# First expert stage of a two-layer graph network: inner units interleaved over the blocks, mixing weights repeated over partitions by a transfer

## The reference

```python
tw = _routing_weights(xf, Wr, br, Wgate, bgate)      # 16 weights of a node, most of them 0
out = jnp.zeros_like(xf)
for e in range(E):                                   # E = 16
    h = jax.nn.silu(xf @ W1[e]) * (xf @ W3[e])       # 32 inner units of one expert
    out = out + tw[:, e:e + 1] * (h @ W2[e])
```

## Time and profile before

| | |
|---|---|
| median of 3 runs (lowest, highest) | 2427.51 us (2425.49, 2428.58) |
| profiled execution: run, span | 2430.37 us, 2428.6 us |
| PE busy over the span | 2278.6 us (94%) |
| DVE, ACT, POOL busy | 1795.1 (74%), 1152.4 (47%), 676.4 (28%) |
| mean granted TensorE clock | 0.969 of 2.4 GHz |
| from 500 to 1100 us: PE, DVE, ACT busy of 600 us | 600.00, 502.08, 317.68 |

### The profile page before, as it was taken

One profiled execution on the slowest core, in us unless ns is written; L12 is line 12 of the kernel. 1 busy time (PEld: TensorE's weight loads), 2 busy tenths in 40 slices (PEclk: granted clock), 3 DMA queues, 4 the chain that ended last, 5 costly groups with the idle time before them and its releaser, 6 DMA issues. The chain is left out here.

```text
span 2428.6 us, 33166 instructions
## 1 busy us (share of the span) xinstructions
PE 2278.6 (94%) x10610; PEld 1824.9 (75%) x10610; DVE 1795.1 (74%) x4258; ACT 1152.4 (47%) x2136; POOL 676.4 (28%) x624
## 2 busy tenths in 40 slices
PE   6799986899999999999789999999997899999998
PEld 4577664688888888888668788888876677777776
DVE  8588796888888888887556755555566688888886
ACT  7565422445455454554442222222235767667652
POOL 6455022222122221210232222122133434333310
PEclk9899987999999999999899999999999899999999
DMA  5221133132231322311453343433446566666631
GB/s 168 57 54 53 19 126 104 57 100 83 75 104 53 105 70 87 102 51 52 135 173 126 125 145 127 134 129 128 135 157 195 123 174 160 148 169 166 152 106 51
DMA packets 155873, 271.89 MB, mean 112 GB/s; under 512 B 35538, under 2 KB 36178, under 8 KB 155478
## 3 DMA queue, kind: packets, MB, share of 16 engines
q1 hardware_dynamic: 123014, 203.00, 25.1%
q0 software_dynamic: 32720, 67.19, 12.9%
HBM read 185.82 MB, written 100.41 MB: 118 GB/s over the span
## 5 line engine op out<-in xcount | busy, mean ns | idle before, releaser
L2417 ACT ACTIVATE conv_h<-conv_h 128x512 f32<-128x512 f32 x79 | 50.0, 632 | 305.9 <-DVE conv_h L2346 288.8
L2894 POOL DMA_INDIRECT next_own<-message,net_slot_d x75 | 123.7, 1650 | 155.4 <-DMA next_own<-own 138.1
L2315 DVE TENSOR_TENSOR conv_yl<-conv_pty,conv_yh 128x512 fp32r<-128x512 f32 x79 | 54.6, 692 | 150.2 <-ACT conv_yh L2407 140.9
L67 PE MATMUL conv_p<-conv_w_hi,conv_yh 128*128 128x512 f32 x316 | 132.2, 418 | 1.2 <-DVE conv_yl L2315 1.2
L1372 POOL TENSOR_TENSOR d_rs<-d_ve,net_half_neg 128x4 f32<-128x4 f32 x37 | 37.3, 1008 | 340.8 <-DVE d_ve L1430 283.4
L67 PE MATMUL d_po<-shared_wq_hi,d_hh 128*128 128x512 f32 x316 | 129.4, 409 | 0.0
L67 PE MATMUL d_pc<-d_xh,shared_wv_hi 128*128 128x512 f32 (+1 forms) x320 | 128.4, 401 | 0.0
L67 PE MATMUL d_pa<-d_xh,xp_w_hi 128*128 128x512 f32 (+1 forms) x320 | 127.6, 399 | 0.0
L69 PE MATMUL conv_p<-conv_w_hi,conv_yl 128*128 128x512 f32 x316 | 126.2, 399 | 0.0
L68 PE MATMUL conv_p<-conv_w_lo,conv_yh 128*128 128x512 f32 x316 | 126.0, 399 | 0.0
L69 PE MATMUL conv_p<-conv_w_hi,conv_hl 128*128 128x512 f32 x316 | 125.5, 397 | 0.0
(11 more groups left out here) (621 smaller groups left out, 7209.5 us busy)
## 6 DMA issues: line engine op xcount, KB each, us to landing
conv_yin<-y SPq DMA_DIRECT2D x79, 256.0 KB, 2.8
h<-conv_h SPq DMA_DIRECT2D x79, 256.0 KB, 2.0
own<-xp_own_buf SPq DMA_DIRECT2D x79, 256.0 KB, 2.0
next_own<-own SPq DMA_DIRECT2D x79, 256.0 KB, 4.3
next_x<-y SPq DMA_DIRECT2D x79, 256.0 KB, 3.8
out<-d_res SPq DMA_DIRECT2D x79, 256.0 KB, 2.7
y<-d_y SPq DMA_DIRECT2D x78, 256.0 KB
d_x<-in_x SPq DMA_DIRECT2D x10, 1024.0 KB, 7.3
```

Source lines behind the costliest of these rows:

```text
L67: te.matmul(out, lhs[0], rhs[0], start=first, stop=False, skip_group_check=True)
L2315: v.tensor_tensor(lo[:, t % 2, :], bank[t % 2][:], hi[:, t % 2, :].bitcast(F32), ALU.subtract)\
L2417: act_.activation(h[:, t, :], h[:, t, :], ACT.Relu).then_inc(h_made, 1)
L2894: pool.indirect_dma_start(own[n][:, t, :], None, k.message2[:, :], bass.IndirectOffsetOnAxis(ap=k.slot["d"][:, T * g + t:T * g + t + 1], a ...
```

## The change

Inner units are dealt out anew: block `cc` now holds units `8cc` to `8cc+7` of every one of the 16 experts, so partition `p` of every block belongs to expert `p // 8`. The columns of `e_w1`, `e_w3` and the rows of `e_w2` are put into that order by the host before the launch (`interleaved`). One 128 x 512 tile of weights, `mix_wide`, then serves all four blocks of a group. It is made so: DVE writes `mix` with 32 places for a tile; PE turns it with one transpose (before, two); ACT copies the 16 x 128 pieces of the four tiles from four quadrants of `d_ptr` to 16 partitions, `mix_rows`, times 0.25 (four copies in place of two); SP starts a transfer that writes each of the 16 rows to 8 partitions of `mix_wide` (`widen_mix`), and DVE multiplies with that tile out of SBUF instead of the bank `d_pmix` (`scale_mix`, split off from `scale_gate`). Gone are `spread` and its bank, the constants `expert`, `expert2`, `expert_r`, and the high and low `parts` of the weights. In block 0 the product with the weights is moved behind the low part of the next group's tile 0.

```diff
+PER = P // EXPERTS0
...
-        mix = c.sb("mix", [P, T, EXPERTS0])
-        parts = c.sb("parts", [P, T, HALF_P], F32R)
-        mix_t = c.sb("mix_t", [P, GR], F32R)
+        mix = c.sb("mix", [P, T, QUAD])
+        mix_rows = c.sb("mix_rows", [EXPERTS0, GR])
+        mix_wide = c.sb("mix_wide", [P, GR])
...
+            def widen_mix(g):
+
+                sp.wait_ge(hidden, KC * g + 2)
+                sp.wait_ge(mix_out, T * g + T)
+                rows = mix_rows[:, cols(g)]
+                sp.dma_start(mix_wide[:, cols(g)], rows.unsqueeze(1).broadcast_to([EXPERTS0, PER, rows.shape[1]]))                  .then_inc(mix_in, 16)
...
+                if c_ and in_range(i, c_, 0):
+                    widen_mix(i * XS + c_)
...
             load(2, 2)
+            widen_mix(0)
             sp.wait_ge(w2_low, 1)
             load(3, 3)
...
-            def constants():
-                s(pool.memset(expert[:], 0.25))
-                s(pool.memset(expert2[:], 0.25))
...
                 v.tensor_tensor(h, h, pc[cc % 2][:, cols(g)], ALU.mult).then_inc(gated, 1)
+
+            def scale_mix(g, cc):
+                h = act_out[:, cc % 2, cols(g)]
                 v.wait_ge(gated, 8 * g + 2 * cc + 2)
-                v.wait_ge(mixed, 4 * g + cc + 1)
-                v.tensor_tensor(h, h, pmix[:, cols(g)], ALU.mult).then_inc(hidden, 1)
+                v.wait_ge(mix_in, 16 * g + 16)
+                v.tensor_tensor(h, h, mix_wide[:, cols(g)], ALU.mult).then_inc(hidden, 1)
...
-                link(ins)
-                v.wait_ge(mix_turned, g + 1)
-                link(v.tensor_copy(parts[:, :, 0:EXPERTS0], mix[:]))
-                s(v.tensor_tensor(parts[:, :, EXPERTS0:2 * EXPERTS0], mix[:], parts[:, :, 0:EXPERTS0].bitcast(F32),
-                                  ALU.subtract))
+                s(ins)
...
                 chunk(g, 0)
                 if mid:
                     low(g + 1, n1, 0)
+                scale_mix(g, 0)
                 low_hidden(g, 0)
...
-            v.wait_ge(consts, 8)
-            v.tensor_tensor(expert_r[:], expert[:], expert2[:], ALU.add).then_inc(expert_made, 1)
-            v.wait_ge(expert_made, 1)
-            v.tensor_copy(expert_r[HALF_P:HALF_P + 2 * EXPERTS0], expert_r[0:2 * EXPERTS0].bitcast(F32)).then_inc(expert_made, 1)
+            v.wait_ge(consts, 2)
...
                 act_.wait_ge(mix_turned, g + 2)
-                for b in range(2):
-                    act_.activation(tile_pairs(mix_t, b)[pair_rows[b]], ptr[pair_rows[b], 0:2 * P].rearrange("p (a n) -> p a n", a=2),
-                                    ACT.Copy).then_inc(mix_out, 1)
+                if g:
+                    act_.wait_ge(hidden, KC * g + 2)
+                for t in range(T):
+                    act_.activation(mix_rows[:, t * P:t * P + P], ptr[t * QUAD:t * QUAD + EXPERTS0, 0:P], ACT.Copy, scale=0.25)\
+                        .then_inc(mix_out, 1)
...
-                if name == "w1":
-                    pe.wait_ge(hidden, 4 * g + cc + 1)
+                if name == "w1" and g + cc > 1:
+                    pe.wait_ge(gated, 8 * g + 2 * cc - 2)
...
-            def spread(g, cc):
-                pe.wait_ge(hidden, 4 * g + cc + 2)
-                pe.matmul(pmix[:, cols(g)], expert_r[:, cc * P:cc * P + P], mix_t[:, cols(g)], start=True, stop=True).then_inc(mixed, 1)
...
-                for a_ in range(2):
-                    last = pe.transpose(ptr[:, a_ * P:a_ * P + P],
-                                        parts[:, 2 * a_:2 * a_ + 2, :].rearrange("p t n -> p (t n)").bitcast(F32), k.ident[:])
-                last.then_inc(mix_turned, 1)
+                pe.transpose(ptr[:, 0:P], mix[:].rearrange("p t n -> p (t n)"), k.ident[:]).then_inc(mix_turned, 1)
...
+    def interleaved(v):
+
+        return v.reshape(D, EXPERTS0, KC, PER).transpose(0, 2, 1, 3).reshape(D, -1)
...
-        "e_w1": np.asarray(L0_ffn_W1).transpose(1, 0, 2).reshape(D, -1),
-        "e_w3": np.asarray(L0_ffn_W3).transpose(1, 0, 2).reshape(D, -1),
-        "e_w2": np.asarray(L0_ffn_W2).reshape(-1, D),
+        "e_w1": interleaved(np.asarray(L0_ffn_W1).transpose(1, 0, 2)),
+        "e_w3": interleaved(np.asarray(L0_ffn_W3).transpose(1, 0, 2)),
+        "e_w2": interleaved(np.asarray(L0_ffn_W2).transpose(2, 0, 1)).T,
```

More of the change, by code:

```diff
@@ L1260, in dense0_phase @@
         wins, ties = (c.sb(n, [P, NS, 4, 4]) for n in ("wins", "ties"))
[L1261 to L1263 removed]
+        mix = c.sb("mix", [P, T, QUAD])
+        mix_rows = c.sb("mix_rows", [EXPERTS0, GR])
+        mix_wide = c.sb("mix_wide", [P, GR])
         pa, pc, po = ([c.ps(f"{n}{i}") for i in range(2)] for n in ("pa", "pc", "po"))
[L1265 removed]
+        ptr = c.ps("ptr")
         turn_bank = [ptr, pa[0], pa[1], pc[0]]
@@ L1272, in dense0_phase @@
         place_made, slots_out, slots_in = c.sem("place_made"), c.sem("slots_out"), c.sem("slots_in")
-        consts, router_made, expert_made, routed_in = (c.sem(n) for n in ("consts", "router_made", "expert_made", "routed_in"))
+        consts, router_made, routed_in = (c.sem(n) for n in ("consts", "router_made", "routed_in"))
+        mix_in = c.sem("mix_in")
         w2_in, w2_high, w2_low = early.weight_in[2], early.weight_high[2], early.weight_low[2]
@@ L1284, in dense0_phase @@
         turned, xh_made, xl_made = (c.sem(n) for n in ("turned", "xh_made", "xl_made"))
-        up_done, gate_done, mixed, tanh_done = (c.sem(n) for n in ("up_done", "gate_done", "mixed", "tanh_done"))
+        up_done, gate_done, tanh_done = (c.sem(n) for n in ("up_done", "gate_done", "tanh_done"))
         gated, hidden, hh_made, hl_made = (c.sem(n) for n in ("gated", "hidden", "hh_made", "hl_made"))
@@ L1293, in dense0_phase @@
         block = stack.enter_context(nc.Block(no_gpsimd_drain=True))
-        NSTAT, NROUTE = 4, 26
+        NSTAT, NROUTE = 4, 24
         SET4 = SETS * 4
@@ L1403, in _ @@
                 gather(1, t)
-            constants()
             power(1, 1)
@@ L1439, in constants @@
                     v.memset(wr[:, :, b * HALF_P + 2 * SET4:(b + 1) * HALF_P].bitcast(F32), 0.0).then_inc(router_made, 1)
-                    v.memset(tile_pairs(mix_t, 1 - b)[pair_rows[b]].bitcast(F32), 0.0).then_inc(router_made, 1)
                 v.tensor_copy(wr[:, :, HALF_P:HALF_P + 2 * SET4], wr[:, :, 0:2 * SET4].bitcast(F32)).then_inc(router_made, 1)
-                v.memset(parts[:, :, 2 * EXPERTS0:HALF_P].bitcast(F32), 0.0).then_inc(router_made, 1)
+                v.memset(mix[:, :, EXPERTS0:QUAD], 0.0).then_inc(router_made, 1)
             def front0_begin(i, c_):
@@ L1590, in routing @@
                 sets = prob[:].rearrange("p (t s) e -> p t s e", t=T)
+                v.wait_ge(mix_turned, g + 1)
                 for t in range(T):
-                    ins = v.tensor_tensor(mix[:, t, :].rearrange("p (s e) -> p s e", e=4), sets[:, t, 1:SETS, :],
+                    ins = v.tensor_tensor(mix[:, t, 0:EXPERTS0].rearrange("p (s e) -> p s e", e=4), sets[:, t, 1:SETS, :],
                                           sets[:, t, 0, :].unsqueeze(2).broadcast_to([P, 4, 4]), ALU.mult)
-                link(ins)
-                v.wait_ge(mix_turned, g + 1)
-                link(v.tensor_copy(parts[:, :, 0:EXPERTS0], mix[:]))
-                s(v.tensor_tensor(parts[:, :, EXPERTS0:2 * EXPERTS0], mix[:], parts[:, :, 0:EXPERTS0].bitcast(F32),
-                                  ALU.subtract))
+                s(ins)
                 assert s.n == NROUTE
@@ L1669, in body @@
                 scale_gate(g, 1)
+                scale_mix(g, 1)
                 low_hidden(g, 1)
@@ L1679, in body @@
                 scale_gate(g, 2)
+                scale_mix(g, 2)
                 if front:
@@ L1689, in body @@
                 scale_gate(g, 3)
+                scale_mix(g, 3)
                 if front and tiles(g + 2) == T:
@@ L1869, in _ @@
             pe.sem_inc(mix_turned, 1)
-            pe.wait_ge(router_made, 6)
+            pe.wait_ge(router_made, 4)
             def turn(g, t, first=False):
@@ L1877, in turn @@
                 elif not first:
-                    pe.wait_ge(mix_out, 2 * g)
+                    pe.wait_ge(mix_out, T * g)
                 for kc in range(KC):
@@ L1937, in body @@
                     turn_mix(0)
-                    pe.wait_ge(expert_made, 2)
-                    pe.wait_ge(mix_out, 2)
-                    spread(0, 0)
                     turn(1, 0)
@@ L1946, in body @@
                     up(g, n, 0, "w3", pc, gate_done)
-                    pe.wait_ge(mix_out, 2 * g + 2)
-                    spread(g, 0)
                     if mid:
@@ L1954, in body @@
                     up(g, n, 1, "w3", pc, gate_done)
-                spread(g, 1)
                 if mid:
@@ L1961, in body @@
                 up(g, n, 2, "w3", pc, gate_done)
-                spread(g, 2)
                 up(g, n, 3, "w1", pa, up_done)
@@ L1966, in body @@
                 up(g, n, 3, "w3", pc, gate_done)
-                spread(g, 3)
```

3 lines of the change are left out of this document (removed).

## The result

| | before | after |
|---|---|---|
| median (lowest, highest) | 2427.54 us (2425.49, 2428.58) | 2449.05 us (2447.04, 2449.52) |
| ratio, 95% interval | | 1.0087 [1.0074, 1.0099] |
| profiled execution: run, span | 2430.37, 2428.6 us | 2449.52, 2447.7 us |
| 500 to 1100 us: PE, DVE, ACT busy | 600.00, 502.08, 317.68 | 576.67, 483.91, 306.92 |

The account below looks back on a forecast made before the run. PE bounds the stage, DVE close behind. 17 groups at +0.31 us (+5.3), group 18 -0.3, start +0.5, last group +2.9 sum to +8.4 us: 2435.9, rounded 2436, against the median 2427.51; range 2414 to 2446.

Parts of the forecast that it names:

- PE's gain: On PE, four `spread` products and one transpose go: -0.99 us a group; 0.40 comes back through DVE, net -0.59.
- L: Time of the weights' transfer from SP's issue to landing, taken as 3.55 us, the middle of 2.8 and 4.3.
- the slow case: Slow end of the likeliest case: L = 4.3, ACT's copies 1.3; +0.9 us more a group, some 2452 us.
- the prediction's own chain: Weights 0.90 us late at DVE's block 0 product delay tile 1's low part, then PE: +0.31 us a group.
- Lateness is paid in full: DVE is in-order, so all 0.90 us of the weights' lateness goes into the group: -0.59 + 0.90 = +0.31 us.
- The two stalls: PE waits for DVE at tile 2's transposes, 0.44 us, and at tile 2 of `down`, 0.86 us.
- the prediction's own sign: A period off 37.7 us plus the weights' lateness would mean that DVE's slack was wrong.
- The ends of the stage: Start +0.5 us, group 18 -0.3, last group +2.9, where nothing covers the transfer.
- The transfer under the cover: Rival: with L between 2.0 and 2.8 the weights come in time; -10.4 us, so 2417; chance 0.30.
- Far slower: Rival: eightfold reading makes L = 7.3, weights 4.65 us late, +4 us a group, 2500 or more; chance 0.06.
- DVE alone as the bound: Rival: DVE, not PE's starts, bounds the stage, so removing products on PE gives nothing; no chance of its own.
- The break-even: The whole change, its last group counted, breaks even at about L = 3.1.

## Why the direction was right and the size was not

**What bounds the kernel, and PE's gain: right.** Without the transfer a group gains 0.70 us, forecast 0.59. Of the 0.99 us that the prediction takes off PE, 0.29 come back, where it has 0.40.

**The transfer's landing: the step that failed.** "Here 16 partitions are read eight times each, so I don't take the quick end but the middle of 2.8 and 4.3: L = 3.55" is the mis-sized term. It is 4.4 us, and what makes it so is where the 16 partitions lie: with the same eightfold reading from the even ones it is 3.0. DVE could have used the weights at 785.34 + 0.60 = 785.94 and got them at 787.56: 1.62 us late, forecast 0.90. Of the difference of 0.72, the landing is 0.85, and 0.14 comes back since the waking on both sides took 0.13 us, not 0.27. ACT's copies, taken at 1.15, are 1.14. The landing lies just above 4.3, the end at which I had priced the slow case. Put through the prediction's own chain, L = 4.4 makes the weights 1.75 us late, a group +1.16, the last one +3.75 and the sum +23.7 us; the profiled spans differ by 19.1. The queue was empty, as assumed, but the load is issued 16 us ahead (767.26 to 783.11), not 20. The rule of the Trainium skill that I had weighed (page "SBUF — State Buffer", section "Door 1: The DMA port swizzle"; L = 3.8) pointed the right way and is short by 0.6 us. From 16 ports to 4, by its rates, the 256 KB take 1.8 us more (0.6 to 2.4, an estimate); 4.4 - 2.3 = 2.1 is measured. And I had set it on a 2.0-us store, where the quickest transfer of this kind lands in 2.3.

**Lateness is paid in full: nearly.** Of 1.62 us, 39.09 - 37.59 = 1.50 are in the period. With the measured lateness the forecast for a group would have been -0.59 + 1.62 = +1.03; it is +0.80, 0.11 by the larger gain of PE and 0.12 by what isn't paid. The two stalls stand where the prediction has them. At tile 2's transposes PE starts at 791.68 instead of 790.24 + 0.23 = 790.47: 1.21 us (forecast 0.44, with the measured lateness 1.16). From the start of `down` to its tile 2 it is 811.78 - 805.59 = 6.19 us instead of 5.62: 0.57 (forecast 0.86). And -0.99 + 1.21 + 0.57 = +0.79. So DVE's slack ahead of `back` was sized 0.3 us too small, which the prediction's own sign says too: the period is 39.09, not 37.7 + 1.62 = 39.3. Beside that, the way of payment was told too simply. I named only the instructions behind the product on DVE; the moved statistics show that the rounding on ACT, and what is queued behind it, hands the lateness on just as surely.

**The chances.** At 0.80 us each in place of 0.31, the 15 groups of the table make 12.0 us where the prediction has 4.7. That is 7.3 of the 9.7 us by which the stage's 18.1 exceed the forecast of 8.4, and it put the time outside the range, which ends at 2446 though the text itself gives 2452 for L = 4.3. The end should have followed that term.

**The ends of the stage.** Start: up to `down` of group 1 the forecast has 0.5 + 0.31 = +0.8, and +1.6 is measured. PE waits 4.86 us for ACT's copies at the start and then 5.04 us for the low part of tile 1, where before it waited 6.6 and 1.08. The waits after, and then the last of the waits before:

```profile
429.71 1.09 PE L1880 MATMUL d_ptr<-net_ident,d_xf 128*128 128x128 f32 x4 [4.86 <-ACT d_mix_rows L1778]
...
438.44 1.09 PE L1880 MATMUL d_ptr<-net_ident,d_xf 128*128 128x128 f32 x4 [5.04 <-DVE d_xl L1480]
```

```profile
437.28 1.09 PE L1880 MATMUL d_ptr<-net_ident,d_xf 128*128 128x128 f32 x4 [1.08 <-DVE d_xl L1483]
```

I had priced the late product, not the low part behind it. Here the clock plays a part too. It is at the 1.2 GHz level in both kernels (granted 0.51 and 0.50 from 430 to 440 us), and holds it longer in the changed one (0.98 against 0.86 from 440 to 450 us): the twelve matmuls between these transposes and the next take 443.68 - 439.18 = 4.50 us, before 441.99 - 438.01 = 3.98. Last group: DVE waits 2.80 us for the transfer, and from the last addition of the group before to the stage's own (1154.10 to 1174.81, and 1168.74 to 1192.91) it is 24.17 us instead of 20.71: +3.5, forecast +2.9:

```profile
1174.43 0.46 DVE L1503 TENSOR_TENSOR d_act_out<-d_act_out,d_mix_wide 128x288 f32<-128x288 f32 x1 [2.80 <-DMA d_mix_wide<-d_mix_rows]
```

**The rivals.** The transfer under the cover was priced at 2417: with the landing of 2.3 us it is 2418.79, and with the transfer gone 2415.32. Its condition (L below 2.65) fits: at 2.3 us DVE doesn't wait for the transfer, at 3.0 it waits 0.23 us a group. The change as made didn't meet it. Far slower was wrong for one transfer. DVE alone as the bound falls with the kernel without the transfer. The break-even, put at L = 3.1, is about right: 3.0 us gives 2423.49 and 4.4 us 2449.05, and a straight line between them meets the kernel before at some 3.2 to 3.3 (an estimate).

**What stays open.** That partitions are tied to ports as the page of the Trainium skill says is not seen in a record of any port; the runs show only that six layouts (adjacent, even, all 128, and the three pairs of halves) order themselves as it says. Whether reading a partition eight times costs something beside that is open. Of the +4.8 us behind `down` of group 16, the 1.3 us that aren't the last group's were not followed up.

## What to carry to other kernels

Before an engine's product is replaced by a transfer, ask which partitions the transfer reads, not only how many bytes it moves: 16 adjacent ones took 4.4 us here, 16 spread over 32 took 3.0. And write down what is queued behind its first reader on every in-order engine, two engines deep. A late value cost next to nothing here once work that doesn't need it stood ahead of its reader on all of them (2417.03 us, against 2415.32 without the transfer); closing one way alone changed nothing. Where the term that decides isn't in the trace, let the range end where that term's own bound puts the time.

## What the runs showed of the hardware

- A transfer of 256 KB from SBUF to SBUF landed in 2.3 us from 128 partitions, 3.0 us from 16 even partitions of 32, and 4.4 us from 16 adjacent ones, each of the 16 read eight times. Two of the last kind, issued 0.6 us apart: 6.5 us for the second.
- Two transfers of 128 KB from 16 rows each, issued 0.6 us apart, have a median landing of 3.7 us if the two sets of rows are 32 partitions apart and of 3.1 us if they are 64 apart.
- ACT's four copies of 16 x 128 out of four quadrants take 1.14 us together, against 0.77 for two of 64 x 256.
- A wait of PE of 3.80 us was followed by 3.4 us at the 1.2 GHz level, one of 1.06 us by none. The long one cost 1.6 us beyond its own length.
